# Loads of x moved from SyncE's queue to ScalarE's, and left operands asked for two steps later

## The reference

```
score = exp((x @ w_a + b_a) @ w_b);  score = PAD where a row of x is all zero
q     = softmax(score, over the 50 rows) weighted sum of x      (twice: w1,b1,w2 and w3,b3,w4)
h     = [q1, q2] @ w5 + b5                                      (300)
f6    = h @ w6 + b6
cross = h[:, iu] * h[:, ju] * (v @ v.T)[iu, ju]                 (44850 pairs)
f7    = cross @ w7 + b7
out8  = [f6, f7] @ w8 + b8
y     = einsum('bu,bku->bk', out8, label_embedding)             (200 scores a user)
```

## Time and profile before

| | |
|---|---|
| median of 3 runs | 1834.8 us (1830.94 to 1834.85) |
| profiled execution: time, span | 1836.85 us, 1835.0 us |
| PE busy | 1587.0 us, 86% of the span |
| DVE busy | 1479.3 us, 81% |
| ACT busy | 921.9 us, 50% |
| DMA, mean over the span | 336 GB/s, 616.99 MB |
| SP's queue (q1), ACT's queue (q10) | 368.24 MB, 244.16 MB |
| chain that ended last | PE 71%, DVE 8%, DMA 8%, ACT 7%, SP 3% |

### The profile page before, as it was taken

One profiled execution on the slowest core, in us unless ns is written; L12 is line 12 of the kernel. 1 busy time (PEld: TensorE's weight loads), 2 busy tenths in 40 slices (PEclk: granted clock), 3 DMA queues, 4 the chain that ended last, 5 costly groups with the idle time before them and its releaser, 6 DMA issues.

```text
span 1835.0 us, 24651 instructions
## 1 busy us (share of the span) xinstructions
PE 1587.0 (86%) x6936; PEld 1148.7 (63%) x6936; DVE 1479.3 (81%) x5519; ACT 921.9 (50%) x2851; POOL 33.3 (2%) x62
## 2 busy tenths in 40 slices
PE   0659999999999999997999999999999999989300
PEld 0236676777777777774777777767777777656200
DVE  8988987764699999978899987748777677498996
ACT  4443375765564646463564634434444444200798
POOL 0000000000000000000000000000000000000000
PEclk9789999999999999998999999999999999999755
DMA  7568966768789899997989999999999899899996
GB/s 283 230 262 317 368 261 247 270 216 287 290 310 419 324 401 368 384 338 303 403 306 414 344 401 409 369 304 386 353 341 344 318 387 356 273 420 421 359 417 246
DMA packets 139214, 616.99 MB, mean 336 GB/s; under 512 B 16432, under 2 KB 43693, under 8 KB 106181
## 3 DMA queue, kind: packets, MB, share of 16 engines
q1 hardware_dynamic: 105157, 368.24, 53.0%
q10 hardware_dynamic: 31744, 244.16, 34.4%
q0 software_dynamic: 2176, 3.01, 0.5%
HBM read 611.55 MB, written 3.79 MB: 335 GB/s over the span
## 4 chain that ended last, share of the span: by engine, by line
PE 71%; DVE 8%; DMA 8%; ACT 7%; SPq 3%; issue 2%; ACTq 0%; POOL 0%; DVEq 0%; POOLq 0%
PE bank L603 64%; ACT stream L753 6%; DMA wring<-in_w7p 5%; DVE junk L830 3%; PE bank L555 3%; DVE stream L946 2%; SPq L442 2%; PE bank L568 2%; DMA sring<-hrows 1%; DVE cring L928 1%; DVE cring L916 1%; ACT absjunk L669 1%; DMA stream<-in_x 1%; PE bank L544 0%; PE bank L614 0%
## 5 line engine op out<-in xcount | busy, mean ns | idle before, releaser
L603 PE MATMUL bank<-wring,cring 128*128 128x300 f32 (+1 forms) x5616 | 1451.6, 419 | 55.9 <-DVE cring L928 19.4
L603 PEld LDWEIGHTS bank<-wring,cring 128*128 128x128 f32 (+1 forms) x5616 | 1065.7, 191 | 424.4 <-DVE cring L916 30.5
L744 ACT ACTIVATE wring<-wring,gcol 128x300 f32<-128x300 f32 x1237 | 564.7, 532 | 613.3 <-DMA wring<-in_w7p 317.9
L946 DVE SCALAR_TENSOR_TENSOR stream<-stream,out 128x300 f32<-128x300 f32 x1335 | 546.0, 465 | 0.8 <-DMA stream<-in_label 0.4
L928 DVE TENSOR_TENSOR cring<-lefts,sring 128x1024 f32<-128x1024 f32 (+2 forms) x309 | 368.1, 1192 | 184.7 <-PE bank L603 182.2
L830 DVE SCALAR_TENSOR_TENSOR junk<-stream,ubc 128x300 bf16<-128x300 f32 x896 | 364.0, 465 | 10.4 <-DMA stream<-in_x 10.4
L669 ACT ACTIVATE absjunk<-stream 128x300 bf16<-128x300 f32 x448 | 196.1, 440 | 44.6 <-PE bank L603 42.6
L555 PE MATMUL bank<-stream,wts 128*32 128x300 f32 x896 | 66.2, 451 | 58.4 <-DVE small L872 58.4
L753 ACT ACTIVATE stream<-stream 128x300 f32<-128x300 f32 x265 | 115.5, 438 | 0.1
L946 DVE DVE_READ_ACCUMULATOR stream<-stream,out 128x1 f32 x1335 | 108.9, 82 | 0.0
L916 DVE SCALAR_TENSOR_TENSOR cring<-lefts,gcol,sring 128x128 f32<-128x128 f32 x334 | 95.0, 345 | 16.0 <-PE bank L603 14.8
(11 more groups left out here) (66 smaller groups left out, 241.3 us busy)
## 6 DMA issues: line engine op xcount, KB each, us to landing
stream<-in_label SPq DMA_DIRECT2D x320, 750.0 KB, 8.2
wring<-in_w7p ACTq DMA_DIRECT2D x184, 1200.0 KB, 8.4
stream<-in_x SPq DMA_DIRECT2D x64, 1050.0 KB, 12.3
sring<-hrows SPq DMA_DIRECT2D x152, 256.0 KB
wring<-in_w7p ACTq DMA_DIRECT2D x9, 1050.0 KB, 9.1
wring<-in_w7p ACTq DMA_DIRECT2D x9, 600.0 KB, 7.7
lefts<-hrows SPq DMA_DIRECT2D x48, 64.0 KB, 6.8
sring<-hrows SPq DMA_DIRECT2D x32, 88.0 KB
```

Of the source, the lines that this page charges most:

```text
L603: mm = pe.matmul(acc[b % 4][:, 0:E], cring[0:rows, p % CSLOTS, b % 2, j0 + j, :], w, start=(p == BEGIN[b] and j == 0), stop=(p == END[b] - ...
L744: ins = nc.scalar.activation(w, w, ACT.Copy, scale=gcol[:, t:t + 1])
L946: ins = nc.vector.scalar_tensor_tensor(out=row_in, in0=row_in, scalar=1.0, in1=out8[:, m % 4, :], op0=ALU.mult, op1=ALU.mult, accum_out=sc ...
```

## The change

From step 0 on, the loads of x are issued by ACT instead of SP, between the softmax's exp and w7_load, at step end+5 of the section that had the slot instead of end+7. In the steps below 0 SP issues them still: for sections 0 and 1 at end+7 as before, for section 2 at end+5, which is step -1 (before: step 1). The wait for `x_used` goes along with each. `STORED` goes from 5 to 7: left operands of the tiles after the first are asked for two steps later. `L_FREE` = 8 takes the place of `X_FREE` = 7 where the labels' steps are worked out: the first seven label loads move from step 96 to 97, and the labels widen to 13 slots from load 133 on instead of 126.

```diff
-    X_FREE = 7
-    STORED = 5
+    L_FREE = 8
+    STORED = 7
...
-    X_WIDE_DONE, X_DONE = DOTS[WIDE - 1][1] + X_FREE, DOTS[NS - 1][1] + X_FREE
+    X_WIDE_DONE, X_DONE = DOTS[WIDE - 1][1] + L_FREE, DOTS[NS - 1][1] + L_FREE
...
+    def x_free(s):
+
+        return DOTS[s][1] + (7 if s < 2 else 5)
...
+        def x_load(queue, n):
+            if X_BEFORE[n] is not None:
+                queue.wait_ge(x_used, X_BEFORE[n] // PARTS + 1)
+            queue.dma_start(xring[:, X_SLOT[n]], x_v[n]).then_inc(x_in[X_SLOT[n]], 16)
...
-            def x_load(n):
-                if X_BEFORE[n] is not None:
-                    sp.wait_ge(x_used, X_BEFORE[n] // PARTS + 1)
-                sp.dma_start(xring[:, X_SLOT[n]], x_v[n]).then_inc(x_in[X_SLOT[n]], 16)
...
             for n in range(XSLOTS):
-                x_load(n)
+                x_load(sp, n)
...
             for q in range(START, STOP):
-                for n in [n for n in range(XSLOTS, NS * PARTS) if DOTS[X_BEFORE[n] // PARTS][1] + X_FREE == q]:
-                    x_load(n)
+                if q < 0:
+                    for n in [n for n in range(XSLOTS, NS * PARTS) if x_free(X_BEFORE[n] // PARTS) == q]:
+                        x_load(sp, n)
...
                 for s in at(SOFT, q):
                     softexp(s)
+                if q >= 0:
+                    for n in [n for n in range(XSLOTS, NS * PARTS) if x_free(X_BEFORE[n] // PARTS) == q]:
+                        x_load(act, n)
                 if 0 <= q < POS:
                     if q in FROM and FROM.index(q) + 2 < len(BLOCKS):
```

## The result

| | kernel before | changed kernel |
|---|---|---|
| median, both run beside each other | 1834.82 us (1830.94 to 1835.33) | 1891.41 us (1889.1 to 1892.17) |
| profiled execution: time, span | 1836.85, 1835.0 us | 1889.1, 1887.3 us |

The ratio is 1.0311, with a 95% interval of 1.0293 to 1.0329: slower by 56.6 us. The forecast was slower, 1883 us, and 1891 lies inside its range. The two traces show 52.3 us of it: the profiled execution of the kernel before was a little slower than its median, that of the changed kernel the fastest of its four.

What follows compares the result with a forecast made beforehand. PE was taken as the bound, busy in nearly every slice, so only gaps of PE after its first product move the end. Terms 12 + 4 + 39 - 7 = +48 gave 1885, 1883 us as median; range 1865 to 1900, with rivals 1845 to 1903.

Steps and rivals of the forecast that it cites:

- head: Kernel start: section 2's x loads go ahead of the first product's right operand, delaying PE; +12 us (+1.3 to +18).
- early x: Before the labels: w7 late behind x on ACT's queue; sections 3, 4, 6 give +3, +2, -1 us (0 to +12).
- late x: Loads of sections 11 to 15 on ACT's queue: w7 lands late and PE stalls; +39 us (0 to +76).
- w7 behind four x at the labels: Sections 11 to 15: w7 lands 22.2 us after ACT's queue reaches x; 29.7 us stalls, 9 us slow starts.
- SP's queue relieved: Hand-built operands near 820 us: without x on SP's queue PE waits less there; -7 us (0 to -11).
- Labels' landing under 15 us: Sign to look for at the x events: label loads land in under 15 us, against 23.4 us with x on SP.
- L_FREE at nothing: Label slots released one step later, widening seven loads later: covered, 0 to +3 us if a label is late.
- STORED at nothing: Left operands asked for two steps later: cover of 18 steps and more, so no cost.
- Rival (a): Order matters at the kernel's start only, w7 lands within 14.4 us elsewhere; 1847 us, chance 0.15.
- Rival (b): Taking x off SP's queue gains near 820 us and about 150 to 315 us, -23; 1816 us, chance 0.05.
- Rival (c): At the five label events stalls cascade, ACT issuing the next w7 late too, 39 more; about 1905 us, chance 0.10.
- rival (d): ACT reaches x late and DVE starves: five events of +4 in place of w7's 39; 1864 us, chance 0.05.

Runs made afterwards that it cites:

- e5: Kernel before with only section 2's four x loads moved to SP's step -1 instead of 1, still on SP's queue: 1847.35 us, ratio 1.0075.
- e3: Changed kernel with the x loads of sections 11 to 15 still on ACT's queue, but one every second step instead of four in one: 1863.43 us, ratio 1.0165.
- e4: Kernel before with only the x loads of sections 11 to 15 moved to ACT's queue, one every second step: 1834.36 us, ratio 0.9999.
- e6: Kernel before with only the x loads of sections 11 to 15 moved to ACT's queue, four in one step: 1862.82 us, ratio 1.0147.
- e10: Kernel before with only the x loads of sections 3, 4 and 6 spread one at a time, still on SP's queue: 1826.81 us, ratio 0.9947.
- e11: Kernel before with the x loads of sections 3, 4 and 6 on ACT's queue, spread one at a time: 1825.14 us, ratio 0.9951.
- e7: Kernel before with only the labels' steps worked out with 8 instead of 7: 1839.88 us, ratio 1.0032.
- e9: Kernel before with only the x loads waiting for sections 3 to 8 (23 loads) on ACT's queue, four in one step: 1844.56 us, ratio 1.0047.

## Why the prediction was right, and where it was off

The parts run alone, by their ratios: head +0.75%, early x +0.47%, late x +1.47%, L_FREE +0.32%, STORED +0.05%, together 3.06% (with their intervals, about 0.5 either way) against the 3.11% of the change. They add up.

- **Head** (forecast 12): 11.9 undone, 12.9 alone. Right, by its mechanism. That PE's first product stands at 120.14 in the changed kernel, close to the forecast's 121, is partly luck: section 2's pooling came 3.9 us earlier in that trace (103.57 against 107.45), and from the first x issue to the product took 16.3 us, where the forecast's rows give 13.9. In e5, with the pooling at 108.11, the product is at 122.78, 14.4 us behind the x issue.
- **w7 behind four x at the labels** (forecast 39, of it 29.7 of stalls and 9 of slow starts): the five jumps sum to 36.9, of it 25.8 of waits and 11.1 of slow starts and smaller gaps. The forecast took the slow start from a row and did not say what it is; the profile has it as the granted clock. Behind the five gaps PE runs for some 20 us in all at 0.50 (until 613.4, 726.1, 825.0, 930.9 and 1046.9), which at half speed costs an estimated 10 us. The price of a load held too: at the fifth event x was issued at 1010.98 behind the w7 of 1010.48 (which landed 8.9 us later, at 1019.4), and the next w7 landed at 1041.1: 21.7 us for four x and one w7, forecast 22.2. The smallest event is the fourth, as forecast (3.11 us of wait, forecast 2.7), and the fifth came as forecast (8.04 for 8.5); the second was to be the largest with 8.7 and had 5.05. The w7 landings were 19.1, 19.5, 18.1, 16.9 and 22.5 us, only one of them the "20 us or more" of the text. The upper end of this term, +76, does not come out of its own prices: 29.7, five times 4 and twice 9 make 68.
- **SP's queue relieved** (forecast -7): the trace has -10.6, the sign and the place right, but this step's reason failed. That the number came near is luck: without the stalls there is no gain (e3, e4).
- **Labels' landing under 15 us** at the x events: it came at two of the five. Five loads issued from 581 to 600 landed a median 20.6 us later, against the 23.4 of the earlier trace rows. Taken over the 20 us from the first x issue on, the medians of the five events are 20, 13, 19, 19 and 11 us, where the kernel before has 23, 21, 24, 23 and 25. So x in the other queue still held the labels up at three of the five events, which speaks against the full -7.
- **Early x** (forecast 4): 10.8 us in the trace of the changed kernel, 8.6 alone. The mechanism was right and the size off. I had put x at 2.5 us each with SP's queue nearly empty. The w7 issued at 157.39 behind four x landed 15.7 us later, at 173.1; the first x of the four was issued at 153.78 and landed 7.4 us later, at 161.2. So three x and a w7 took 11.9 us, where 2.5 us a load of x (1050 KB) and 2.9 for w7 make 10.4. With a spare of 8.1 us that is 7.6 us late, not 6. Section 6's -1 was +2.2 (PE waits 3.0 us for the scaled w7 there, before 2.5).
- **L_FREE at nothing** (forecast 0, with +3 at most): +5.5. This is the one term put at nothing that is not. I looked at when the first label is due, not at what a later burst of label loads runs into: hand-built operands in the same queue, some 80 us on. The row that told of it was the earlier trace rows, a wait of 2.32 us already there.
- **STORED at nothing**: right.

The forecast fell 8 us short. By the parts run alone, early x cost 4.6 us and L_FREE 5.5 us more than forecast and the head 0.9 more, while late x, with what came back at the hand-built operands, cost 28.4 instead of 39 - 7 = 32.

Rival (a) fell with e6: w7 did land later than its spare. Rival (b) named two gains: the one at 820 isn't one, and that between 150 and 315 us is to be had by spreading, on either queue (e10, e11), and not by the move. Rival (c), stalls that double, didn't show: PE's jumps are no larger than the wait and its slow start. Of rival (d) there is no sign: the new waits end with w7 or with what stands behind it, and DVE waited 5.3 us for x in all, before 10.4.

The Trainium skill, "DMA: Bandwidth & Descriptors", section "Issuing engines are not separate DMA queues", says that a second issuing engine only saves the sequencer's time; by that the sum would have ended at the head alone. For loads spread over the steps the runs agree with it (e4 0.9999, and e10 beside e11). For four in one step they do not (e6 1.0147).

## What to carry to other kernels

Before a bulk load is moved into another engine's queue, work out for the small-slack load that stands next in that queue when it lands behind the whole burst; if that is beyond its spare, issue the burst one load at a time, which cost nothing here (e4) and was worth more than the choice of queue (e10, e11). A gain that shows in the trace of a kernel that also stalls more is to be tried without the stalls. A step that only delays a prefetch still moves a burst: look at what it meets where it lands, not at when it is first needed.

## What the runs showed of the hardware

- With both queues full, landings in one queue come at an even pace: at the first and the fifth label event x (1050 KB) every 4.3 to 4.9 us and the w7 (1200 KB) behind them 4.7 and 4.2 us after the last, near the 4.4 and 4.7 worked out from the earlier trace rows. With SP's queue nearly empty three x and a w7 took 11.9 us, about 374 GB/s by their 4350 KB (of 1024 bytes).
- Issues become slow on an engine whose queue is backed up: 1.65 us for three small loads where labels landed in 4.4 us, 6.84 for the same three where they took 17.9; 4.58 us for six where labels took 5 to 10 us (issued at 1204), 10.12 for the same six where they took 12 to 15 (issued at 1217, e7).
- PE is slow just behind a gap, and the granted clock says why: 0.50 at 1043 to 1046 us, behind 8.04 us without a matmul, and 1.00 from 1049 on, with PE busy throughout (changed kernel); in the kernel before 0.50 from 826.3 to 836.5, in and behind the gap of the earlier trace rows. By time, 16 records took 5.77 us in e9 right after 7.39 us of idle time, and 4.31 us in e3 after 0.56.
